# A one-core block of attention-like mixing and a gated network: TensorE makes 53 unread products in the waits of the first two groups

## The chip, the cores and the metric

The kernel runs on one core of a Trainium2 chip. The metric is the device time of one execution, in microseconds (us); lower is better. TensorE (PE) multiplies, VectorE (DVE), ScalarE (ACT) and GpSimd (POOL) work elementwise, SyncE (SP) issues transfers.

## What is computed

The input `x` has 32 sequences of 256 tokens with 128 channels, in f32. Each token row is normalized; then comes a block with two halves, and then a feed-forward network, each with a normalization behind it and a residual:

```python
x = x + _layernorm(_L0_attn_ref(_layernorm(x), ...))
x = x + _layernorm(_L0_ffn_ref(_layernorm(x), ...))

# _L0_attn_ref
x = x + lif(time_mix(layer_norm(x, ln1_s, ln1_b), ...))
x = x + lif(channel_mix(layer_norm(x, ln2_s, ln2_b), ...))
# time_mix: mixes each token with the one before, k = xk @ Wk, v = xv @ Wv,
#   sigmoid(xr @ Wr) * wkv(w_decay, u_first, k, v) @ Wo     (wkv: a scan over time)
# channel_mix: sigmoid(xr @ Wr) * (square(relu(xk @ Wk)) @ Wv)     (Wk 128x512, Wv 512x128)
# lif: a scan over time that emits spikes where a voltage reaches 1
# _L0_ffn_ref: h = silu(x @ w1) * (x @ w2); h = gelu(h @ h1); h = gelu(h @ h2); h @ w3
```

The weights of the feed-forward network are -1, 0 and 1 with a scale for each output.

## The kernel before

The 32 sequences are cut into 16 groups of two, 512 tokens each. A group is held with tokens on the partitions for normalizations and turned on TensorE to channels on the partitions for products and scans over time. Each engine has an instruction stream of its own, written out by hand as *turns*. In turn i the engines work on several groups at once: on group i the input norm, on i-1 the time mix, on i-2 its output and the channel mix, on i-3 and i-4 the feed-forward network. `g[k]` in the code is group i-k, and `on[k]` says whether there is one. Turns below 3 run `first_turn`, those from 3 on `turn`, the last ones `last_turn`; turns 6 to 13 are a loop. Engines wait for each other by semaphores, and an engine never runs ahead of an instruction of its own that waits.

On TensorE a group passes these steps (the names are those of the code and of the text below):

- `turn_1` transposes the normalized tokens (`n1`) into the bank `p_turn`; ScalarE makes `z1` of it, GpSimd the difference `d1`, VectorE the three inputs `mixed1`.
- `k_product`, `r_product_1`, `v_product`: f32 products of 512 columns. VectorE scans `p_k` (`maximum`, `excess`), ScalarE takes exponentials, VectorE and GpSimd scan and multiply, and at the end VectorE writes `yr`.
- `out_product` multiplies `yr` with Wo; ScalarE copies it to `h_in[0]`, VectorE scans the voltage and marks spikes, `fired_sum(0)` asks whether any neuron fired, GpSimd branches on it, `spikes_turned(0)` transposes the spikes back.
- `turn_2` transposes the second norm (`n2`); ScalarE makes `z2`, GpSimd `d2`, VectorE `mixed2`. Then `r_product`, `channel_k` 0 to 3 (ScalarE: `relu`, `square`) and `channel_v` 0 to 3. Behind `r_product` ScalarE takes tanh and loads the table of exponentials, then comes `relu` 0.
- `channel_v` 3 ends the channel mix; VectorE makes `h_in[1]` of it and scans it, and then come `fired_sum(1)` and `spikes_turned(1)`.
- `turn_4`, `to_gate`, `to_value`, `hidden` and `last_product` are the feed-forward network, whose weights are split into a rounded part `w_hi` and a rest `w_lo`.

TensorE's program exists twice from turn 3 on: with products of `w_lo`, and without them where all of `w_lo` is 0. At the end of turn 2 TensorE sums the maxima of the rest (`rest_sum`), VectorE copies the sum to `w_rest_all`, and TensorE reads it and branches:

```python
program(False, last=2)
...
long_weights = pe.value_load(w_rest_all[0:1, 0:1].bitcast(I32))
with pe.If(long_weights != 0):
    program(True, first=3)
with pe.Else():
    program(False, first=3)
```

The weights of the mixes lie in `mix`, blocks 0 to 2 being Wk, Wv and Wr; the third transfer that SP issues brings blocks 0 to 4 (`s_mix_in`), and the next one brings `kk`, 1 MB of the other weights. `p_f` are two banks for results of the feed-forward network; before that network starts, `p_f[1]` holds the scales of w3 (until `s_w3_scaled`), and `p_f[0]` receives `rest_sum`.

Of the kernel before, what the change touches and what calls it, by code (L numbers as in the profile page):

```python
# [31 lines left out]
P = 128  # L32
# [39 lines left out]
def build(nc, x_in, vec_in, scale_in, mix_in, ffn_in, out):  # L72
# [13 lines left out]
    with ExitStack() as ctx:  # L86
# [1348 lines left out]
        def _(pe):  # L1435
# [3 lines left out]
            def program(general, **turns):  # L1439
# [5 lines left out]
                def turn_1(g):  # L1445
                    pe.wait_ge(s_n[1], g.n + 1)
                    after(pe, s_f_out, g.n - 4)
                    if isinstance(g.n, int):
                        after(pe, s_f0_lo, g.n - 3)
                        after(pe, s_z2, g.n - 2)  # L1450
                        after(pe, s_z1, g.n - 1)
                    turned(1, g, n1)

                def turn_2(g):
                    pe.wait_ge(s_n[2], g.n + 1)
                    after(pe, s_z1, g.n + 1)
                    if isinstance(g.n, int):
                        after(pe, s_f_out, g.n - 3)
                        after(pe, s_f0_lo, g.n - 2)
                        after(pe, s_z2, g.n - 1)  # L1460
                    turned(2, g, n2)
# [17 lines left out]
                def k_product(g):  # L1479

                    after(pe, s_h_in[0], g.n - 1)
                    if isinstance(g.n, int):
                        after(pe, s_e, g.n - 1)
                    time_product(g, 0, "Wk", p_k, s_k)
# [21 lines left out]
                def out_product(g):  # L1506

                    after(pe, s_e, g.n)
                    if isinstance(g.n, int):
                        after(pe, s_h_in[0], g.n - 1)  # L1510
                    pe.wait_ge(s_yr, g.n + 1)
                    if isinstance(g.n, int) and g.n == 0:
                        pe.wait_ge(s_quarter[0], 1)
                    pe.matmul(p_k[:, :], mix[:, MIX["Wo"]], flat(yr[:, :, :]), start=True, stop=True).then_inc(s_wo, 1)

                def fired_sum(k, g):

                    if k == 0:
                        after(pe, s_fired_all[1], g.n - 1)
                        if isinstance(g.n, int):  # L1520
                            after(pe, s_h_in[1], g.n - 1)
                            after(pe, s_relu, g.n - 1, HB, 3)
                            after(pe, s_relu, g.n - 1, HB, 1)
                            after(pe, s_tanh_r, g.n)
                            after(pe, s_fired_all[0], g.n - 1)
                    elif k == 1:
                        after(pe, s_h_in[1], g.n)
                        if isinstance(g.n, int):
                            after(pe, s_relu, g.n, HB, 3)
                            after(pe, s_relu, g.n, HB, 1)  # L1530
                            after(pe, s_tanh_r, g.n + 1)
                            after(pe, s_fired_all[0], g.n)
                            after(pe, s_fired_all[1], g.n - 1)
                    pe.wait_ge(s_fired[k], g.n + 1)
                    pe.matmul(p_m[0][:, 2 * k:2 * k + 1], ones16[:, :], fired[k][:, :], start=True,
                              stop=True).then_inc(s_fired_sum[k], 1)

                def spikes_turned(k, g):

                    if k == 0:  # L1540
                        after(pe, s_x3, g.n - 1)
                        if isinstance(g.n, int):
                            after(pe, s_x2, g.n - 1)
                    elif k == 1:
                        after(pe, s_x2, g.n)
                        if isinstance(g.n, int):
                            after(pe, s_x3, g.n - 1)
                    pe.wait_ge(s_spikes[k], g.n + 1)
                    tile = flat(spikes[k][:, :, :])
                    for j in range(J):  # L1550
                        last = pe.transpose(p_spk[:, k, j * P:(j + 1) * P], tile[:, j * P:(j + 1) * P], ident16[:, :])
                    last.then_inc(s_spk_tok[k], 1)
# [229 lines left out]
                def last_product(g):  # L1782
# [10 lines left out]
                                             start=(m == 0), stop=(m == HB - 1))  # L1793
                    last.then_inc(s_w3, 1)

                def rest_sum():

                    pe.wait_ge(s_rest1, 1)
                    pe.matmul(p_f[0][:, 0:1], ones16[:, :], w_rest1[:, :], start=True,
                              stop=True).then_inc(s_rest_sum, 1)  # L1800

                def first_turn(g, on):

                    if on[2]:
                        out_product(g[2])
                        fired_sum(0, g[2])
                        spikes_turned(0, g[2])
                    if on[1]:
                        k_product(g[1])
                    if on[2]:  # L1810
                        turn_2(g[2])
                    if on[1]:
                        r_product_1(g[1])
                    if on[2]:
                        r_product(g[2])
                    if on[1]:
                        v_product(g[1])
                    if on[2]:
                        channel_k(g[2], 0)
                        channel_k(g[2], 1)  # L1820
                        channel_k(g[2], 2)
                        channel_v(g[2], 0)
                        channel_k(g[2], 3)
                        channel_v(g[2], 1)
                        channel_v(g[2], 2)
                    if on[0]:
                        turn_1(g[0])
                    if g[0].n == 2:
                        rest_sum()

                def turn(g, on):

                    if on[4]:
                        to_gate(g[4], 3)
                        to_value(g[4], 3)
                    if on[3]:
                        channel_v(g[3], 3)
                    if on[2]:
                        out_product(g[2])
                    if on[4]:  # L1840
                        hidden(1, g[4], 0)
                        hidden(1, g[4], 1)
                    if on[3]:
                        fired_sum(1, g[3])
                    if on[4]:
                        hidden(1, g[4], 2)
                    if on[3]:
                        spikes_turned(1, g[3])
                    if on[2]:
                        fired_sum(0, g[2])  # L1850
                    if on[4]:
                        hidden(1, g[4], 3)
                    if on[2]:
                        spikes_turned(0, g[2])
                    if on[1]:
                        k_product(g[1])
                    if on[4]:
                        hidden(2, g[4], 0)
                        hidden(2, g[4], 1)
                        hidden(2, g[4], 2)  # L1860
                    if on[2]:
                        turn_2(g[2])
                    if on[1]:
                        r_product_1(g[1])
                    if on[4]:
                        hidden(2, g[4], 3)
                    if on[2]:
                        r_product(g[2])
                    if on[1]:
                        v_product(g[1])  # L1870
                    if on[2]:
                        channel_k(g[2], 0)
                    if on[3]:
                        turn_4(g[3])
                    if on[2]:
                        channel_k(g[2], 1)
                        channel_k(g[2], 2)
                    if on[4]:
                        last_product(g[4])
                    if on[3]:  # L1880
                        to_gate(g[3], 0)
                    if on[2]:
                        channel_v(g[2], 0)
                        channel_k(g[2], 3)
                    if on[3]:
                        to_value(g[3], 0)
                        to_gate(g[3], 1)
                    if on[2]:
                        channel_v(g[2], 1)
                        channel_v(g[2], 2)  # L1890
                    if on[3]:
                        to_value(g[3], 1)
                        to_gate(g[3], 2)
                    if on[0]:
                        turn_1(g[0])
                    if on[3]:
                        to_value(g[3], 2)
# [115 lines left out]
```

## Time and profile before

| | |
|---|---|
| median of 3 runs | 709.31 us (706.81 to 709.71) |
| profiled execution | 710.65 us |
| its span | 708.5 us |
| mean granted clock of TensorE | 0.949 |
| TensorE busy | 613.5 us (87%), 2563 products |
| VectorE, ScalarE, GpSimd busy | 566.3, 482.4, 438.4 us |
| TensorE's longest waits up to 100 us | 15.0 us in 4 for `n` (L1442), 11.0 in 1 for `yr`, 5.3 in 1 with the releaser "issue" |

The span is the time from the first to the last instruction of the profiled execution; the device time holds 2.15 us more. Busy time counts products on TensorE and no weight loads; products overlap in the pipeline, so ends of products are later than the start of the next. The granted clock is 1.00 at full speed (2.4 GHz) and 0.50 at half (1.2 GHz). A row names engine, line of the kernel, operation and its tiles, output first. A product of f32 operands stands as two instructions.

### The profile page before, as it was taken

To read this page: it belongs to the slowest core of one execution; us is meant where nothing else is said; L and a number is where in the kernel's file an instruction comes from. 1 tells how busy PE (TensorE), PEld (TensorE's weight loads), DVE (VectorE), ACT (ScalarE), POOL (GpSimd) and SP (SyncE) were. 2 spreads that over 40 slices of the span, in tenths; PEclk is the share of its full clock that TensorE was granted. 3 is DMA by queue.
4 is the path that set the end of the run, shared out by engine and by line. 5 is a ranking of instruction groups with operands and counts; after the bars stand their busy time and mean duration, and the time that the engine had idled before them with its cause. 6 is when DMAs were issued, how large, how long until landed. Compare 5 with 4: busy or idle time off the path is not lost. (4 is left out here: it accounts for less than half of the span.)

```text
span 708.5 us, 10945 instructions
## 1 busy us (share of the span) xinstructions
PE 613.5 (87%) x2563; PEld 399.0 (56%) x2563; DVE 566.3 (80%) x1552; ACT 482.4 (68%) x718; POOL 438.4 (62%) x560
## 2 busy tenths in 40 slices
PE   1245589999999999999999999999999999999884
PEld 0012236666656566666666666656666666566753
DVE  3866779898989999998989898989889897936230
ACT  3636076877869595959687786959595968757261
POOL 4333454687877767676768677786767684635242
PEclk9758579999999999999999999999999999999897
DMA  7000000001010000001010101000000101000000
GB/s 271 23 8 16 1 15 17 16 15 31 16 31 17 30 16 12 18 15 30 15 30 15 30 15 30 15 30 16 17 15 1 30 1 31 16 0 16 1 15 16
DMA packets 26538, 16.82 MB, mean 24 GB/s; under 512 B 1152, under 2 KB 25728, under 8 KB 26240
## 3 DMA queue, kind: packets, MB, share of 16 engines
q1 hardware_dynamic: 26496, 16.34, 7.6%
q8 instruction: 17, 0.28, 0.2%
q14 instruction: 25, 0.20, 0.1%
HBM read 12.14 MB, written 4.19 MB: 23 GB/s over the span
## 5 line engine op out<-in xcount | busy, mean ns | idle before, releaser
L735 ACT ACTIVATE hid<-p_f,scale 128x512 f32<-128x512 f32 x128 | 86.6, 687 | 102.0 <-PE p_f L1634 101.7
L1634 PE MATMUL p_f<-b_lo,w_hi 128*128 128x512 f32 x256 | 114.0, 445 | 11.0 <-DVE b_lo L306 10.9
L1634 PE MATMUL p_f<-a_lo,w_hi 128*128 128x512 f32 x256 | 112.5, 440 | 2.8 <-DVE a_lo L306 1.0
L449 POOL TENSOR_TENSOR nd<-factors,pq 128x512 f32<-128x512 f32 x32 | 38.0, 1187 | 102.1 <-DVE pq L1065 102.1
L1634 PE MATMUL p_f<-a_hi,w_hi 128*128 128x512 f32 x256 | 101.0, 394 | 0.0
L1634 PE MATMUL p_f<-b_hi,w_hi 128*128 128x512 f32 x256 | 101.0, 394 | 0.0
L433 POOL TENSOR_TENSOR rstd<-var,minus_half 128x4 f32<-128x4 f32 x64 | 75.0, 1172 | 2.5
L1619 PE MATMUL p_m<-kk,mix 128*128 128x512 f32 x128 | 64.0, 602 | 9.5 <-issue 5.3
L1634 PEld LDWEIGHTS p_f<-b_lo,w_hi 128*128 128x128 f32 x256 | 48.1, 188 | 37.5 <-issue 25.7
L1792 PEld LDWEIGHTS p_turn<-w,hid 128*128 128x128 f32 x512 | 61.5, 200 | 12.3 <-DVE f_lo L1173 11.0
L1792 PE MATMUL p_turn<-w,hid 128*128 128x128 f32 x512 | 63.9, 285 | 2.3 <-DVE f_lo L1173 1.4
L420 POOL TENSOR_TENSOR var<-mv,eps_row 128x4 f32<-128x4 f32 x64 | 35.0, 547 | 48.4 <-DVE mv L985 48.3
L1603 PE MATMUL p_m<-mixed,mix 128*128 128x512 f32 x128 | 63.6, 600 | 0.0
L1634 PEld LDWEIGHTS p_f<-a_lo,w_hi 128*128 128x128 f32 x256 | 48.2, 188 | 27.0 <-issue 8.6
L1634 PEld LDWEIGHTS p_f<-b_hi,w_hi 128*128 128x128 f32 x256 | 48.2, 188 | 15.0 <-issue 6.2
L441 POOL TENSOR_SCALAR f_out<-f_out,neg_mean,rstd 128x128 f32<-128x128 f32 x64 | 55.0, 871 | 0.8 <-POOL rstd L433 0.8
L1634 PEld LDWEIGHTS p_f<-a_hi,w_hi 128*128 128x128 f32 x256 | 48.3, 189 | 11.2 <-issue 3.6
L1094 DVE TENSOR_TENSOR_SCAN volt<-half_row,h_in 128x256 f32<-128x256 f32 x64 | 50.4, 827 | 2.8 <-ACT h_in L686 2.8
L1442 PE MATMUL p_turn<-ident,n 128*128 128x128 f32 x192 | 31.0, 286 | 16.6 <-DVE n L1001 16.5
L729 ACT ACTIVATE a_hi<-hid 128x512 fp32r<-128x512 f32 x64 | 40.6, 635 | 6.8 <-DVE hid L1184 6.2
L441 POOL TENSOR_SCALAR x<-xa,neg_mean,rstd 128x128 f32<-128x128 f32 x64 | 45.0, 712 | 0.3 <-POOL rstd L429 0.2
L1442 PEld LDWEIGHTS p_turn<-ident,n 128*128 128x128 f32 x192 | 23.3, 145 | 36.6 <-DVE n L1001 31.8
(135 smaller groups left out, 1506.8 us busy)
## 6 DMA issues: line engine op xcount, KB each, us to landing
xa<-in_x SPq DMA_DIRECT2D x16, 256.0 KB, 2.9
xb<-in_x SPq DMA_DIRECT2D x16, 256.0 KB, 2.9
out<-y_out SPq DMA_DIRECT2D x16, 256.0 KB, 3.0
kk<-in_ffn SPq DMA_DIRECT2D x1, 1024.0 KB, 7.1
hid<-in_ffn SPq DMA_DIRECT2D x1, 1024.0 KB, 9.6
mix<-in_mix SPq DMA_DIRECT2D x1, 512.0 KB, 6.5
gate<-in_ffn SPq DMA_DIRECT2D x1, 512.0 KB, 5.6
mix<-in_mix SPq DMA_DIRECT2D x1, 320.0 KB, 3.8
```

The costliest lines, as they stand in the source:

```text
L420: pool.tensor_tensor(var[n][:, :], mv[n][:, :, 1], eps_row[:, :], ALU.add).then_inc(s_var[n], 1)
L433: pool.tensor_tensor(rstds[n][:, :], var[n][:, :], minus_half[:, 0], ALU.pow).then_inc(s_rstd[n], 1)
L441: last = pool.tensor_scalar(out_[:, j], in_[:, j], neg_mean[n][:, j:j + 1], rstd[:, j:j + 1], ALU.add, ALU.mult)
L449: pool.tensor_tensor(nd[:, n], factors[:, 0], pq[:, n, :, 0:T], ALU.mult).then_inc(s_apq, 1)
L729: act.activation(dst[:, m], hid[:, m], ACT.Copy).then_inc(s_hi[layer], 1)
L735: act.activation(hid[:, m], p_f[m % 2][:, :], ACT.Gelu, scale=scale[:, 1 + layer, m:m + 1]).then_inc(s_gelu[layer], 1)
L1094: last = dve.tensor_tensor_scan(volt[k][:, b], half_row[:, :], h_in[k][:, b], 0.0, ALU.mult, ALU.add)
L1442: last = pe.transpose(p_turn[:, j * P:(j + 1) * P], tiles[:, j], ident[:, :])
L1603: pe.matmul(p_m[m % 2][:, :], mix[:, MIX["fWk"] + m], flat(mixed2[:, 1]), start=True, stop=True).then_inc(s_fk, 1)
L1619: last = pe.matmul(p_m[0][:, :], mix[:, MIX["fWv"] + m], kk[:, m], start=(m == 0), stop=(m == HB - 1))
L1634: last = pe.matmul(out_, w[:, b], x[:, k], start=(k == 0 and t == 0), stop=(k == n - 1 and t == len(terms) - 1))
L1792: last = pe.matmul(p_turn[:, j * P:(j + 1) * P], hid[:, m, j * P:(j + 1) * P], w3[:, m], start=(m == 0), stop=(m == HB - 1))
```

## The change

A new helper `busy` makes products of the weights with themselves into a bank of `p_f` that nobody reads at that time, 384 columns each, for groups 0 and 1 alone, at fourteen places of `first_turn` and `turn`. It waits for the weights, and in turn 3 and later also for the scaling of w3. No other engine is touched, and no result depends on these products.

```diff
+                def busy(g, counts, k):
+
+                    if isinstance(g.n, int) and g.n in counts:
+                        pe.wait_ge(s_mix_in, 16)
+                        if k:
+                            pe.wait_ge(s_w3_scaled, 1)
+                        for _ in range(counts[g.n]):
+                            pe.matmul(p_f[k][:, 0:3 * P], mix[:, 0], flat(mix[:, 0:3]), start=True, stop=True)
...
                 def first_turn(g, on):
 
                     if on[2]:
+                        busy(g[2], {0: 15}, 0)
                         out_product(g[2])
+                        busy(g[2], {0: 3}, 0)
                         fired_sum(0, g[2])
+                        busy(g[2], {0: 1}, 0)
                         spikes_turned(0, g[2])
                     if on[1]:
+                        busy(g[1], {0: 7}, 0)
                         k_product(g[1])
                     if on[2]:
+                        busy(g[2], {0: 5}, 0)
                         turn_2(g[2])
...
                     if on[2]:
+                        busy(g[2], {0: 1}, 0)
                         r_product(g[2])
...
                         channel_k(g[2], 2)
+                        busy(g[2], {0: 2}, 0)
                         channel_v(g[2], 0)
...
                     if on[0]:
+                        busy(g[0], {1: 3}, 0)
                         turn_1(g[0])
...
                     if on[3]:
+                        busy(g[3], {0: 6}, 1)
                         channel_v(g[3], 3)
...
                     if on[3]:
+                        busy(g[3], {0: 1}, 1)
                         fired_sum(1, g[3])
...
                     if on[3]:
+                        busy(g[3], {0: 2}, 1)
                         spikes_turned(1, g[3])
...
                     if on[2]:
+                        busy(g[2], {1: 1}, 1)
                         spikes_turned(0, g[2])
...
                     if on[2]:
+                        busy(g[2], {1: 5}, 1)
                         turn_2(g[2])
...
                     if on[2]:
+                        busy(g[2], {1: 1}, 1)
                         r_product(g[2])
```

What this makes of TensorE's order at the start, from the first `k_product` (L1476, `p_k`) to the first `out_product` (L1514). L1803 is the unread product, and a row with x7 stands for seven in a row; the lines below the helper move down by 9.

```order
+L1803 MATMUL p_f<-mix 128x384 x7
 L1476 MATMUL p_k<-mixed,mix 128x512
 L1476 MATMUL p_m<-mixed,mix 128x512
 L1476 MATMUL p_v<-mixed,mix 128x512
-L1442 MATMUL p_turn<-ident,n 128x128 x4
+L1803 MATMUL p_f<-mix 128x384 x3
+L1442 MATMUL p_turn<-ident,n 128x128 x4
+L1803 MATMUL p_f<-mix 128x384 x15
 L1514 MATMUL p_k<-yr,mix 128x512
```

Seven unread products now stand between group 0's first transposes and its k product, three ahead of the transposes of group 1, and fifteen ahead of the output product; the order of all others is as before.

The second place is the end of turn 2 and the start of turn 3, in group 0. L1799 (now L1808) is `rest_sum`, the next two rows load the flag and branch on it, L1619 is `channel_v` 3 and L1514 the output product of group 1.

```order
-L1799 MATMUL p_f<-w_rest,ones 128x1
-L1974 TENSOR_LOAD w_rest_all
-L1975 COMPARE_AND_BRANCH
+L1808 MATMUL p_f<-w_rest,ones 128x1
+L1997 TENSOR_LOAD w_rest_all
+L1998 COMPARE_AND_BRANCH
+L1803 MATMUL p_f<-mix 128x384 x6
 L1619 MATMUL p_m<-kk,mix 128x512
 L1514 MATMUL p_k<-yr,mix 128x512
```

The six unread products stand behind the branch, at the head of the code that it jumps to, and ahead of `channel_v` 3.

## Rows read from the trace of the kernel before

**Rows 1.** The page: TensorE's granted clock in 40 slices, in tenths.

```profile
PEclk9758579999999999999999999999999999999897
```

**Rows 2.** Stretches: us; busy us of PE, PEld, DVE, ACT, POOL; clock; DMA; GB/s.

```profile
65.50:100.00 34.50, 17.09 (x41) 7.28 (x40) 24.77 (x76) 12.22 (x18) 14.73 (x21) 0.65 0.06 17
...
130.00:650.00 520.00, 499.04 (x2165) 329.69 (x2166) 457.54 (x1250) 393.27 (x595) 360.55 (x443) 1.00 0.06 18
```

**Rows 3.** Timeline of TensorE: start us, us, engine, line, operation, [idle before <-releaser].

```profile
10.12 1.11 PE L1442 MATMUL p_turn<-ident,n 128*128 128x128 f32 x4 [4.17 <-DVE n L1001]
16.35 2.07 PE L1476 MATMUL p_k<-mixed,mix 128*128 128x512 f32 x2 [5.12 <-DVE mixed L1021]
18.21 1.91 PE L1476 MATMUL p_m<-mixed,mix 128*128 128x512 f32 x2
19.92 1.91 PE L1476 MATMUL p_v<-mixed,mix 128*128 128x512 f32 x2
24.52 0.66 PE L1442 MATMUL p_turn<-ident,n 128*128 128x128 f32 x4 [2.69 <-DVE n L1001]
36.19 2.04 PE L1514 MATMUL p_k<-yr,mix 128*128 128x512 f32 x2 [11.01 <-DVE yr L1088]
41.05 0.16 PE L1535 MATMUL p_m<-fired,ones 128*128 128x1 bf16 x1 [2.82 <-DVE spikes L1102]
42.64 0.61 PE L1551 MATMUL p_spk<-ident,spikes 128*128 128x128 bf16 x4 [1.43 <-POOLq L488]
...
48.86 1.12 PE L1442 MATMUL p_turn<-ident,n 128*128 128x128 f32 x4 [3.80 <-DVE n L1001]
...
52.75 2.07 PE L1565 MATMUL p_m<-mixed,mix 128*128 128x512 f32 x2 [1.07 <-DVE mixed L1139]
...
70.86 2.04 PE L1619 MATMUL p_m<-kk,mix 128*128 128x512 f32 x2 [5.32 <-issue]
...
90.77 2.05 PE L1565 MATMUL p_m<-mixed,mix 128*128 128x512 f32 x2 [1.35 <-DVE mixed L1139]
```

**Rows 4.** The same timeline where the granted clock is full.

```profile
62.37 1.02 PE L1603 MATMUL p_m<-mixed,mix 128*128 128x512 f32 x2
63.22 1.88 PE L1619 MATMUL p_m<-kk,mix 128*128 128x512 f32 x4
64.94 0.60 PE L1442 MATMUL p_turn<-ident,n 128*128 128x128 f32 x4
```

**Rows 5.** Short stretches, columns as in rows 2: where the clock changes.

```profile
56.20:56.30 0.10, 0.10 (x1) 0.00 (x0) 0.10 (x2) 0.10 (x1) 0.00 (x0) 0.55 0.00 0
93.80:94.00 0.20, 0.20 (x1) 0.00 (x1) 0.20 (x3) 0.20 (x1) 0.20 (x1) 0.91 0.00 0
100.00:105.00 5.00, 5.00 (x11) 2.66 (x10) 3.49 (x10) 3.95 (x7) 2.88 (x3) 0.66 0.00 0
```

**Rows 6.** Timeline of ScalarE and VectorE up to group 0's relu.

```profile
9.44 1.91 ACT L626 ACTIVATE w_hi<-kk 128x2048 fp32r<-128x2048 f32 x1 [5.39 <-DMA kk<-in_ffn]
...
18.45 1.26 DVE L1028 TENSOR_TENSOR_SCAN o<-decay_row,p_k 128x256 f32<-128x256 f32 x2 [0.84 <-PE p_k L1476]
...
55.48 1.28 ACT L657 ACT_TABLE_LOAD   x1
...
57.37 0.60 ACT L704 ACTIVATE kk<-p_m 128x512 f32<-128x512 f32 x1 [0.61 <-PE p_m L1603]
```

**Rows 7.** TensorE's queue at the branch, and the copy of the flag before it.

```profile
65.61 0.15 DVE L1114 COPY w_rest_all<-p_f 1x1 f32<-1x1 f32 x1 [0.21 <-PE p_f L1799]
...
L1975 PEldq COMPARE_BRANCH  x1: 4246/4246/4246, 66.4 to 66.4; - x1
```

**Rows 8.** Timeline of VectorE, GpSimd and ScalarE in group 1.

```profile
75.58 1.27 DVE L1094 TENSOR_TENSOR_SCAN volt<-half_row,h_in 128x256 f32<-128x256 f32 x2
...
88.61 1.04 POOL L459 TENSOR_TENSOR d<-z 128x512 f32<-128x512 f32 x1
...
95.14 0.60 ACT L704 ACTIVATE kk<-p_m 128x512 f32<-128x512 f32 x1 [0.39 <-PE p_m L1603]
```

## The prediction

> **What bounds the kernel now.** I read the page first, then the stretches, then the timeline of the first 105 us. The page's clock line [rows 1] shows TensorE's granted clock well below full speed in slices 2 to 6 (17.7 us each), and full from there almost to the end. The stretches [rows 2] show why: from 130 to 650 us TensorE is busy 499 of 520 us, while from 65.5 to 100 us it is busy 17.1 of 34.5 us at a mean clock of 0.65. So the middle is set by TensorE, and the start by a chain in which the engines hand one group of 512 tokens to each other. An edit of the start is worth what it moves the point at which TensorE stops waiting; the middle carries this shift to the end.
>
> The timeline shows what a product costs at either level. Two f32 products of 512 columns that follow each other start 1.71 us apart in the cold part (18.21 and 19.92 in [rows 3]) and 0.85 us apart at full clock (62.37 and 63.22 in [rows 4]): 1.2 and 2.4 GHz. One by itself ends after 2.04 to 2.07 us, or after 1.02. (The clock view says 1.00 before 25.5 us, where it has recorded no change yet; I go by the durations, which there are those of 1.2 GHz.) An unread product has 384 columns, three quarters: **1.28 us at 1.2 GHz, 0.64 at 2.4**, one behind the other.
>
> How soon does the clock rise? In the unbroken run from 52.75 it came up at 56.25 [rows 3, 5], 3.5 us in; in the run from 90.77 at about 93.8, 3.05 us in [rows 3, 5]; in the run from 16.35 to 21.83 not within 5.5 us, though the transposes at 24.52 took 0.66 us instead of 1.11 [rows 3]. Call c the time at 1.2 GHz after such a run begins: n unread products take 0.64n + c/2. I take c = 4.5, the middle, with ends 3.1 and 5.5, and "not at all" as the outer one.
>
> **The change, step by step.** Nothing is removed. 37 unread products go into group 0's waits and 16 into the next stretch, 53 by the order of instructions. They matter by what they delay and by the clock.
>
> *Seven ahead of the first k product.* TensorE is free at about 11.2 and waits until 16.35 [rows 3]. The weights that they read don't hold them: the load queued behind that one on SP had landed by 9.44 [rows 6]. They need 4.48 + 2.25 = 6.7 us, end at 17.9, and the k product starts 1.6 late. It then takes 1.02 instead of 2.07, so its result is late by 0.5 (-0.15 at c = 3.1, +1.0 at c = 5.5). VectorE's scan at 18.45 waits for it [rows 6], and from there DVE, ACT and POOL pass the work on until yr, which releases the product at 36.19 [rows 3]. Term: **+0.5**.
>
> *Three and fifteen more.* The fifteen need 9.6 us at 2.4 GHz and lie in a wait of 11.0 (before 36.19 in [rows 3]); cover enough unless the clock drops in the wait before them. Term: 0; with a drop 9.6 + 2.25 = 11.85, so up to 0.9 late.
>
> *Group 0's products at 2.4 GHz.* The next small ones (3, 1, 5, 1) need 1.9, 0.6, 3.2 and 0.6 us and lie in waits of 2.8, 1.4, 3.8 and 1.1 [rows 3]: nothing. What they keep up is the clock, and four operations on the chain shrink: the output product at 36.19 by 1.0, the transposed spikes at 42.64 by some 0.2 (an estimate, a third of 0.61), the transposes at 48.86 from 1.12 to 0.60 [rows 3, 4], so 0.5. The channel's first product, at 52.75, then starts at 52.75 + 0.5 - 1.7 = 51.55. Before, the ACT table load behind it ended at 56.76, 4.01 us after its start, and relu at 57.37 still waited 0.61 for TensorE's channel_k [rows 6]. With this product 1.05 shorter the table is in 2.96 us after its start, at 54.5; channel_k ends after 0.85 + 0.85 + 1.02 = 2.7 us, at 54.3. So relu moves from 57.37 to 54.5: **-2.9** after group 0.
>
> *The six behind the branch.* Here the wait isn't what it looks like. TensorE idles until 70.86, released by "issue", not by an operand [rows 3]. The row of the branch shows why: DVE copies the flag at 65.61, and COMPARE_BRANCH holds TensorE's queue for 4246 ns from 66.4, to 70.65 [rows 7]. The six products stand behind that branch in the program, so they can't fill its wait; they start when it ends, and channel_v stands behind them. The branch moves with the chain, to an end at 68.0. After 5 us of nothing the clock is down, as it was before (the product at 70.86 took 2.04). Six products take 3.84 + 2.25 = 6.1 us; channel_v starts at 74.1 and ends at 2.4 GHz at 75.1, against 72.90 before: **+2.2** (+1.5 at c = 3.1; all six at 1.2 GHz take 7.7, which gives +3.8).
>
> A rule against the row: the Trainium skill (Advanced Engine Details and Errata, Control Flow Timing) gives a compare-and-branch about 108 ns, and another of its pages (Runtime: NRT & Kernel Launch, Instruction fetch mechanics) says that a taken branch to a target beyond the fetched instructions stalls until they are fetched. The 4246 ns agree with the second and not with the first; by the first the branch would end 4.1 us sooner in both kernels and the six would cost the same, behind it.
>
> *Group 1.* From channel_v's end DVE works without a pause to the second voltage scan at 75.58 [rows 8], so all of it arrives there. Two sets of transposed spikes give back 0.2 each: +1.8. The small groups (1, 2, 1, 5, 1) fit into their waits. The transposes at 86.59 would be 0.5 shorter, but the shift at 88.61 stands behind POOL's earlier work and not behind them [rows 8]: 0. The channel's product moves from 90.77 to 92.6; again the table is in 2.96 later, at 95.5, where relu began at 95.14 [rows 8]: **+0.4**.
>
> *After that* the same rows follow. In the kernel before the clock sank once more, to a mean of 0.66 in 100 to 105 us [rows 5]. I cost this at nothing either way, since silu and relu of that stretch, on ACT, wait for its own chain; if TensorE is what sets it, up to 1.7 us hang on it, in either kernel.
>
> Sum: +0.5 - 1.7 - 1.7 + (2.2 + 2.9) - 0.4 - 1.4, which is +0.4. (The second -1.7 is the shorter channel product and the 0.61 of waiting for channel_k; the -1.4 is the same in group 1; the bracket is 6.1 us of products less 1.0 for channel_v.) The profiled execution took 710.65 us, 2.15 of it around the span: 711.05. It lies 1.34 above the median of 709.31, so the median should be **709.7**.
>
> The Trainium skill (TensorE: Matmul & The Clock Gate, What's actually happening) puts the whole ramp penalty below 1% of a typical kernel's span; that would cap any gain here at 7.1 us. The rows agree: all that TensorE runs cold on the chain is worth less.
>
> **Rivals.**
> 1. *The six products are hidden*, because the branch's wait or something later swallows them. Then channel_v starts at 68.0 and ends at 69.0, 3.9 earlier than before; 0.4 for the spikes, and relu of group 1 at 90.77 - 4.3 + 2.96 = 89.4, so -5.7: 703.6. For it: a wait of 5.3 us stands there, and later slack on TensorE isn't excluded. Against it: the row of the branch, and that no operand is named as releaser of the product at 70.86. The Trainium skill's advice (TensorE: Matmul & The Clock Gate, Why this matters for your kernels) to leave TensorE no long gaps points this way.
> 2. *The clock rises at once behind the branch.* Then the six take 3.84, channel_v ends as before, and relu comes at 90.37 + 2.96 = 93.3: -1.8, 707.5. Against it: no run of products in the rows rose within 3 us.
> 3. *The clock rises late at both dense places* (slower). It decides from about c = 7 on. All seven at 1.2 GHz take 8.96, the k product stays cold, +3.8; less 1.7; relu at 57.8, +0.4. The branch ends at 71.3, six at 1.2 GHz take 7.7, channel_v cold ends at 81.0, +8.1; relu of group 1 at 98.5 + 2.96, +6.3: 715.6. For it: the 5.5 us from 16.35. Against it: the two rises after 3 to 3.5 us.
> 4. *Unread products don't raise the clock.* Then all 53 run at 1.2 GHz and overrun their waits by 3.8, 8.2, 1.0, 2.6, 7.7, 0.8 and 2.1, about 26 us: 736. Against it: they are the same kind of f32 product as those under which it rose.
>
> **How the numbers follow.** The forecast, within its bounds, has 0.70: c = 3.1 at both places gives -0.95, a late rise of the second +2.5, and three runs of before already differ by 2.9 us, so its own range is 707 to 713. Rival 1 has 0.12, rival 2 0.04, rival 3 0.11, rival 4 0.03. What this measurement can tell from no change is about 0.5%, 3.5 us: faster 0.12, same 0.74, slower 0.14. The range 706.6 to 713.2 leaves out the rivals 1, 3 and 4 for the most part.
>
> **What the profile after would show.** Right: the k product starts at 17 to 18.5; the output product takes 1.02; relu of group 0 comes near 54.5; COMPARE_BRANCH takes over 4 us, and six unread products start within 0.3 us of its end, the first ones 1.28 apart; channel_v starts 5.4 to 7.7 us behind it; relu of group 1 near 95.5. Wrong: a branch row that overlaps these products, or unread products still 1.28 apart in the wait ahead of the output product. The forecast fails most easily in c, which counts at both dense places, and in whether the clock holds through the idle 2 us between them.

## The result: 0.46% slower, by the six products behind the branch

The changed kernel takes 710.97 us (median of 9 runs, 709.72 to 712.33), the kernel before 707.66 (9 runs, 706.47 to 709.71). The ratio is 1.0046, with a 95% interval of 1.0031 to 1.0061: 3.3 us slower, inside the forecast range and below what I had called a difference from no change, but clear of the noise of nine runs. The forecast was +0.4 us. Its 709.7 us lie within 1.3 us of the measured median by luck: they start from the median of the first three runs of before (709.31), and nine runs gave 707.66. The profiled execution after has a span of 709.9 us.

The page of the changed kernel, which answers to [rows 1]: busy time and share of TensorE, and its clock in 40 slices.

```profile
PE 640.7 (90%) x2669; PEld 415.6 (59%) x2669; DVE 566.2 (80%) x1552; ACT 482.7 (68%) x718; POOL 437.2 (62%) x560
...
PEclk9998999999999999999999999999999999999998
```

The change did what its words say: the clock is near full in the slices where it was at 5 to 8 tenths. The unread products stand in the busy time, 640.7 instead of 613.5 us, and say nothing about speed. The stretches, which answer to [rows 2]:

```profile
65.50:100.00 34.50, 25.57 (x69) 12.19 (x69) 20.26 (x63) 6.90 (x10) 12.87 (x18) 0.85 0.03 10
...
130.00:650.00 520.00, 498.92 (x2163) 329.09 (x2162) 458.82 (x1257) 393.84 (x596) 360.14 (x443) 1.00 0.06 19
```

From 65.5 to 100 us TensorE is busy 25.6 instead of 17.1 us at a mean clock of 0.85 instead of 0.65; the middle is as before, 498.9 of 520 us. Next, the timeline of TensorE, answering to [rows 3]; L1803 is the unread product, two instructions for each.

```profile
10.99 7.08 PE L1803 MATMUL p_f<-mix 128*128 128x384 f32 x14
17.91 1.02 PE L1476 MATMUL p_k<-mixed,mix 128*128 128x512 f32 x2
...
25.52 11.54 PE L1803 MATMUL p_f<-mix 128*128 128x384 f32 x30
36.90 1.02 PE L1514 MATMUL p_k<-yr,mix 128*128 128x512 f32 x2
...
48.35 0.65 PE L1442 MATMUL p_turn<-ident,n 128*128 128x128 f32 x4 [1.48 <-DVE n L1001]
...
51.78 1.13 PE L1565 MATMUL p_m<-mixed,mix 128*128 128x512 f32 x2 [0.94 <-DVE mixed L1139]
...
68.10 7.01 PE L1803 MATMUL p_f<-mix 128*128 128x384 f32 x12 [5.08 <-issue]
74.94 1.02 PE L1619 MATMUL p_m<-kk,mix 128*128 128x512 f32 x2
...
93.54 1.27 PE L1565 MATMUL p_m<-mixed,mix 128*128 128x512 f32 x2 [2.02 <-DVE mixed L1139]
94.60 1.92 PE L1476 MATMUL p_v<-mixed,mix 128*128 128x512 f32 x2
```

The seven begin at 10.99, end at about 17.9 and push the k product from 16.35 to 17.91; it takes 1.02 us. The fifteen fill the wait ahead of the output product to its end (36.90), which then takes 1.02 instead of 2.04. The six begin at 68.10, and channel_v stands behind them at 74.94. At 93.54 the channel's first product of group 1 meets a clock that falls: it takes 1.27, and the v product behind it 1.92. The queue of TensorE at the branch, answering to [rows 7], min/median/max in ns and its start:

```profile
L1998 PEldq COMPARE_BRANCH  x1: 3998/3998/3998, 63.9 to 63.9; - x1
```

It ends at 67.9, and the six start 0.2 us later. The two relu on ScalarE that end the steps of the forecast, answering to [rows 6, 8]:

```profile
54.85 0.60 ACT L704 ACTIVATE kk<-p_m 128x512 f32<-128x512 f32 x1
...
98.08 0.60 ACT L704 ACTIVATE kk<-p_m 128x512 f32<-128x512 f32 x1 [1.34 <-PE p_m L1603]
```

Group 0 gained 2.5 us here (57.37 to 54.85), group 1 lost 2.9 (95.14 to 98.08). What this is worth at the end can be read off all profiled executions. The columns are starts of relu 0 of either group, the branch's end, the span, and the span less relu of group 1:

| kernel | relu, group 0 | branch ends | relu, group 1 | span | difference |
|---|---|---|---|---|---|
| before | 57.37 | 70.6 | 95.14 | 708.5 | 613.4 |
| before, second profile | 57.04 | 69.8 | 94.63 | 706.2 | 611.6 |
| changed | 54.85 | 67.9 | 98.08 | 709.9 | 611.8 |
| changed, second | 53.19 | 65.9 | 95.78 | 707.6 | 611.8 |
| changed, third | 53.48 | 66.5 | 96.28 | 708.2 | 611.9 |
| without the six | 54.16 | 66.9 | 89.72 | 701.1 | 611.4 |
| only the six | 57.45 | 70.8 | 98.42 | 710.0 | 611.6 |
| seven ahead of the branch | 52.99 | 65.6 | 88.26 | 699.8 | 611.5 |
| twelve behind it | 54.71 | 67.8 | 101.75 | 713.1 | 611.4 |
| group 0 alone | 54.25 | 67.3 | 90.40 | 702.0 | 611.6 |
| four first | 52.42 | 64.9 | 87.80 | 699.9 | 612.1 |
| four ahead of the branch | 54.26 | 67.0 | 90.61 | 702.5 | 611.9 |
| four and four | 52.46 | 65.3 | 87.24 | 698.9 | 611.7 |
| the same, two more | 52.80 | 65.5 | 87.39 | 697.9 | 610.5 |

In twelve of fourteen the rest of the kernel took 611.4 to 612.1 us: what happens up to relu of group 1 arrives at the end in full. The two others differ by the clock at the end of the kernel: a set of transposed products (L1792) there took 6.78 us in the first profile of before, 5.3 to 5.5 in the twelve, and 3.84 in the last kernel. No added product stands there; why the clock differs there is not shown.

### The profile page after: what moved, and what is told of

It is laid out like the page before. It is cut to its first block and busy times, and to the rows that moved or that the text cites. A ratio compares the mean times of both kernels' runs of the same rounds, so it can differ in the third digit from the quotient of the medians.

```text
span 709.9 us, 11163 instructions
## 1 busy us (share of the span) xinstructions
PE 640.7 (90%) x2669; PEld 415.6 (59%) x2669; DVE 566.2 (80%) x1552; ACT 482.7 (68%) x718; POOL 437.2 (62%) x560
## 5 line engine op out<-in xcount | busy, mean ns | idle before, releaser
L1792 PEld LDWEIGHTS p_turn<-w,hid 128*128 128x128 f32 x512 | 60.1, 196 | 12.8 <-DVE f_lo L1173 11.5
L1619 PE MATMUL p_m<-kk,mix 128*128 128x512 f32 x128 | 62.9, 593 | 2.9 <-ACT kk L704 2.9
L1792 PE MATMUL p_turn<-w,hid 128*128 128x128 f32 x512 | 62.8, 282 | 2.3 <-DVE f_lo L1173 1.4
L1803 PE MATMUL p_f<-mix 128*128 128x384 f32 x106 | 43.8, 563 | 5.1 <-issue 5.1
L729 ACT ACTIVATE b_hi<-hid 128x512 fp32r<-128x512 f32 x64 | 40.5, 632 | 2.0
```

Of the source, the lines that this page charges most:

```text
L729: act.activation(dst[:, m], hid[:, m], ACT.Copy).then_inc(s_hi[layer], 1)
L1619: last = pe.matmul(p_m[0][:, :], mix[:, MIX["fWv"] + m], kk[:, m], start=(m == 0), stop=(m == HB - 1))
L1792: last = pe.matmul(p_turn[:, j * P:(j + 1) * P], hid[:, m, j * P:(j + 1) * P], w3[:, m], start=(m == 0), stop=(m == HB - 1))
L1803: pe.matmul(p_f[k][:, 0:3 * P], mix[:, 0], flat(mix[:, 0:3]), start=True, stop=True)
```

## The experiments

Each kernel is compared with the kernel before on the same chip; the timed ones ran 6 to 12 times. The median of before was 707.39 us beside the first four, 706.86 beside the next four (group 0 alone, four first, four ahead, four and four) and 708.11 beside the last one and the three further profiles, so ratios compare across these and medians don't.

**Without the six.** One line of the changed kernel goes:

```diff
                     if on[3]:
-                        busy(g[3], {0: 6}, 1)
                         channel_v(g[3], 3)
```

> The changed kernel without the six unread products behind the branch; the other 47 stay. Theory (the six stand behind the branch and are pure delay, 6.8 us of products less about 1 us for the faster channel_v): the branch ends near 68.1 us, channel_v starts there, takes 2.04 us at 1.2 GHz and ends near 70.1 instead of 76.0. The small groups behind it then run cold and give back 1 to 2 us, so relu of group 1 comes 4 to 5 us earlier than the 98.1 of the changed kernel, near 93.5: about 706.5 us, ratio to before 0.995 to 1.000. Rival (the six are hidden, and the loss comes from the seven ahead of the k product or from the small groups): no change against the changed kernel, 711 us, ratio 1.0046.

Measured: 702.55 us against 707.39, ratio 0.9933 (0.9912 to 0.9954). Its timeline of TensorE behind the branch, and the branch:

```profile
67.07 2.05 PE L1619 MATMUL p_m<-kk,mix 128*128 128x512 f32 x2 [4.74 <-issue]
68.91 1.91 PE L1514 MATMUL p_k<-yr,mix 128*128 128x512 f32 x2
...
86.68 1.10 PE L1565 MATMUL p_m<-mixed,mix 128*128 128x512 f32 x2 [0.33 <-DVE mixed L1139]
```

```profile
L1997 PEldq COMPARE_BRANCH  x1: 3670/3670/3670, 63.2 to 63.2; - x1
```

channel_v starts at 67.07, 0.2 us behind the branch's end, and takes 2.05 at 1.2 GHz. Even so relu of group 1 comes at 89.72, 3.8 us sooner than I expected: from the branch's end to relu it takes 22.8 us, with the six 30.2. The difference of 7.4 is the 6.84 of the products, less 1.0 for the faster channel_v, plus 1.5: here the channel's first product (86.68) ran at full clock and relu followed in 3.04 us, in the changed kernel in 4.54. The theory stands; I had set its gain too low, and the ratio lies below the 0.995 to 1.000 that I expected.

**Only the six**, in the kernel before: the reverse, all other calls of `busy` removed.

```diff
-                        busy(g[2], {0: 15}, 0)
                         out_product(g[2])
-                        busy(g[2], {0: 3}, 0)
                         fired_sum(0, g[2])
...
                         busy(g[3], {0: 6}, 1)
                         channel_v(g[3], 3)
```

> The kernel before with the six unread products behind the branch alone. Theory: group 0 is as before, the branch ends near 70.7, the six take 6.1 to 7.7 us, channel_v ends 4 to 5.5 us later than the 72.9 of before, and the warmer clock behind it gives back 0.5 to 1.5 us: +3 to +5 us, near 711.7, ratio 1.004 to 1.007. Rival (the six are hidden): 707.7, ratio 1.000.

Measured: 711.63 us, ratio 1.0070 (1.0043 to 1.0098). TensorE behind the branch:

```profile
70.96 5.69 PE L1803 MATMUL p_f<-mix 128*128 128x384 f32 x12 [5.34 <-issue]
76.49 1.02 PE L1619 MATMUL p_m<-kk,mix 128*128 128x512 f32 x2
...
95.38 1.10 PE L1565 MATMUL p_m<-mixed,mix 128*128 128x512 f32 x2 [1.35 <-DVE mixed L1139]
```

The six take 5.53 us from 70.96 to 76.49, and channel_v ends at 77.5, 4.6 later than in [rows 3]. They alone make the kernel slower by at least as much as the whole change does; the two intervals overlap.

The same six cost less here than in the changed kernel. From the branch's end to relu of group 1 it takes 27.6 us with them and 24.5 and 24.8 in the two profiles of before, about 3 more; in the changed kernel it takes 29.8 to 30.2, and 22.8 without them, about 7 more. The cost is not a fixed one: here the channel's first product (95.38) still ran at full clock, 1.10 us, and relu followed in 3.04, while in the changed kernel the clock was falling or low there.

**Twelve behind the branch.**

```diff
-                        busy(g[3], {0: 6}, 1)
+                        busy(g[3], {0: 12}, 1)
```

> The changed kernel with twelve instead of six behind the branch. Theory (pure delay at full clock for each further product): 6 x 0.64 = 3.84 us more, 714.8 us, ratio to before 1.010. Rival (a wait swallows them up to some number): less than 1 us more.

Measured: 714.32 us, ratio 1.0090 (1.0063 to 1.0118).

```profile
67.90 10.73 PE L1803 MATMUL p_f<-mix 128*128 128x384 f32 x24 [5.02 <-issue]
78.47 1.02 PE L1619 MATMUL p_m<-kk,mix 128*128 128x512 f32 x2
```

Twelve take 10.57 us, 3.73 more than six, and relu of group 1 comes 3.67 later. The ratio goes from 1.0046 to 1.0090, which is 3.1 us; the two intervals just stay apart. No wait swallows any.

**Seven ahead of the branch**, none behind it:

```diff
                     if g[0].n == 2:
                         rest_sum()
+                        busy(g[0], {2: 7}, 1)
...
-                        busy(g[3], {0: 6}, 1)
                         channel_v(g[3], 3)
```

> The changed kernel, but the six behind the branch replaced by seven right ahead of it, after the sum of the flag. Theory (the branch holds TensorE's queue of instructions, not the array, so that products issued before it run meanwhile): the seven take 4.5 us from 62.9 to 67.4, COMPARE_BRANCH still ends near 68.1, channel_v and the output product start there at full clock; against the changed kernel channel_v ends 6.9 us earlier, relu of group 1 near 91 to 92: about 704.5 us, ratio 0.994 to 0.997. Rival (the load of the flag waits until the array is empty, so that the products delay the branch): the branch ends at about 72.5 and channel_v starts 1 to 2 us later than that of before, which gives 710 to 711 us.

Measured: 703.25 us, ratio 0.9951 (0.9935 to 0.9967). The timeline, the branch, and two stretches (columns as in [rows 2]):

```profile
61.02 4.76 PE L1803 MATMUL p_f<-mix 128*128 128x384 f32 x14
65.76 1.10 PE L1619 MATMUL p_m<-kk,mix 128*128 128x512 f32 x2
68.65 1.02 PE L1514 MATMUL p_k<-yr,mix 128*128 128x512 f32 x2 [1.79 <-issue]
```

```profile
L1998 PEldq COMPARE_BRANCH  x1: 3498/3498/3498, 62.1 to 62.1; - x1
```

```profile
66.00:67.00 1.00, 0.86 (x2) 0.22 (x2) 0.11 (x1) 0.00 (x0) 0.00 (x0) 1.00 0.05 16
67.00:68.00 1.00, 0.00 (x0) 0.00 (x0) 0.97 (x2) 0.00 (x0) 0.00 (x0) 1.00 0.00 0
```

The seven run from 61.0 to 65.8 while the branch, from 62.1, holds the queue of instructions to 65.6: this branch stops the issue and not the array. So this wait can be filled, from its other side. channel_v starts at once and at full clock. But the output product behind it starts only at 68.65, with the releaser "issue", though its operand `yr` had been written by 64.6, and a queue of instructions fetches 16 KB from 66 to 67 us. I read this as TensorE being out of instructions. VectorE's second voltage scan waited for this product, until 70.33, and the gain of the faster channel_v was gone. From the branch's end to relu it takes 22.7 us, as without the seven, and the intervals of the two ratios overlap.

**Four ahead of the branch** instead of seven, to move this edge.

```diff
-                        busy(g[0], {2: 7}, 1)
+                        busy(g[0], {2: 4}, 1)
```

> As the run with seven products right ahead of the branch, with four. In that run the output product behind channel_v started only 2.9 us after it, with the releaser issue, while 16 KB of instructions were being fetched. Theory (the fetch of the next block of instructions stalls TensorE's queue, and 12 instructions fewer move the edge of the block behind the output product): the output product follows channel_v within 0.9 us at full clock, h_in of group 1 comes 1.8 us sooner relative to the branch's end, relu of group 1 at 21 us behind the branch's end instead of 22.7: near 701.5 us, ratio 0.990 to 0.993. Rival (the stall comes a fixed time after the branch whatever stands there): the output product still starts 3 us after the branch's end, 703.

Measured: 704.46 us, ratio 0.9951 (0.9933 to 0.9970), not better than seven and outside the 0.990 to 0.993 expected.

```profile
67.19 1.10 PE L1619 MATMUL p_m<-kk,mix 128*128 128x512 f32 x2 [2.08 <-issue]
68.12 1.02 PE L1514 MATMUL p_k<-yr,mix 128*128 128x512 f32 x2
...
85.85 2.05 PE L1565 MATMUL p_m<-mixed,mix 128*128 128x512 f32 x2 [1.18 <-DVE mixed L1139]
```

The output product now follows channel_v in 0.93 us, so the stall went with the 12 instructions (a product is two MATMUL and two LDWEIGHTS in the trace). But the channel's first product (85.85) took 2.05 us, and relu came 4.8 us behind it: the clock had fallen there, as in the changed kernel. That the stall goes is shown. What it was worth can be read from the branch's end to the start of the channel's first product: 19.6 us with seven, 18.9 here, and 18.9 and 18.8 in the last two kernels, so some 0.8 us, and the clock took more than that here.

**Group 0 alone**: the 37 products of turns 1 and 2, none from turn 3 on.

```diff
-                        busy(g[3], {0: 6}, 1)
                         channel_v(g[3], 3)
...
-                        busy(g[3], {0: 1}, 1)
                         fired_sum(1, g[3])
...
-                        busy(g[3], {0: 2}, 1)
                         spikes_turned(1, g[3])
...
-                        busy(g[2], {1: 1}, 1)
                         spikes_turned(0, g[2])
...
-                        busy(g[2], {1: 5}, 1)
                         turn_2(g[2])
...
-                        busy(g[2], {1: 1}, 1)
                         r_product(g[2])
```

> The changed kernel with the unread products of turns 1 and 2 alone (37), none from the branch on. Theory: group 0 gains as in the changed kernel (relu of group 0 near 54.5, branch end near 67.5), and from the branch on everything is cold as in the kernel before, where relu of group 1 came 24.5 us after the branch's end, against 22.85 without the six but with the small groups. So relu of group 1 near 92, 3 us earlier than before: about 704.2 us, ratio 0.994 to 0.997. Rival (the gain of the run without the six comes from the small groups of group 1): ratio 0.999 to 1.000.

Measured: 703.71 us, ratio 0.9945 (0.9930 to 0.9961), as expected. The small groups from turn 3 on are worth nothing that this can tell: without the six and with them the ratio was 0.9933, and the intervals overlap.

**Four ahead of the first k product** instead of seven, none behind the branch.

```diff
-                        busy(g[1], {0: 7}, 0)
+                        busy(g[1], {0: 4}, 0)
...
-                        busy(g[3], {0: 6}, 1)
```

> The changed kernel without the six behind the branch, and with four instead of seven ahead of the first k product. Theory (seven overrun their wait by 1.6 us, of which the faster k product gives back 1.05): four take at most 5.1 us from 11.0, end by 16.1, the k product starts at 16.35 as before and, with the clock up by then or soon, ends 0.5 to 1.0 us sooner than with seven: 702.0 us, ratio to before 0.991 to 0.993. Rival (three products less, and the clock comes up later or falls sooner): the k product at 16.35 still takes 2.0 us, and nothing is gained or lost against seven, 702.5.

Measured: 703.22 us, ratio 0.9941 (0.9925 to 0.9957).

```profile
10.99 4.89 PE L1803 MATMUL p_f<-mix 128*128 128x384 f32 x8
15.72 1.02 PE L1476 MATMUL p_k<-mixed,mix 128*128 128x512 f32 x2
```

The four end at 15.72, the k product starts there and takes 1.02. The ratio lies outside the 0.991 to 0.993 expected. With four, relu of group 0 came at 52.42, 52.46 and 52.80 in three kernels, with seven between 52.99 and 54.85 in eight profiles.

VectorE's `mixed1`, the operand of the k product, itself starts between 14.17 and 15.57 us in the fourteen profiles, so the step is read better from that start to the start of `yr`. It is 19.8 us in the three profiles with nothing ahead of the k product, 19.3 to 20.9 with seven (20.2 on average) and 18.8 to 19.2 with four (19.0). By this four are 1.2 us better than seven and 0.8 better than none, while seven lose 0.4 on average. The ratios, 0.9941 here and 0.9933 with seven, don't show it.

**Four and four**: four ahead of the k product, four ahead of the branch, none behind it.

```diff
-                        busy(g[1], {0: 7}, 0)
+                        busy(g[1], {0: 4}, 0)
...
                         rest_sum()
+                        busy(g[0], {2: 4}, 1)
...
-                        busy(g[3], {0: 6}, 1)
```

> Both: four ahead of the first k product and four right ahead of the branch, none behind it. Theory: the two gains add, 701 us, ratio 0.989 to 0.992. Rival (the clock falls in the gaps that the smaller groups leave): no better than 702.5, the run without the six.

Measured: 702.39 us, ratio 0.9927 (0.9906 to 0.9949), just outside the 0.989 to 0.992 expected. Relu of group 1 comes at 87.24, but the intervals of this kernel and of the one without the six overlap; that the gains add isn't shown.

**The same with two more** (three instead of one), to hold the clock in the wait ahead of the channel's first product of group 1:

```diff
                     if on[2]:
-                        busy(g[2], {1: 1}, 1)
+                        busy(g[2], {1: 3}, 1)
                         r_product(g[2])
```

> Four ahead of the k product, four ahead of the branch, none behind it, and three instead of one in the wait ahead of the channel's first product of group 1. Theory (in the changed kernel the clock fell at 94.4 us because TensorE was nearly idle in the 4 us ahead of that product; it then took 4.5 us from its start to relu instead of 2.96): relu follows in 2.9 to 3.1 us here, relu of group 1 at 87 us or sooner, about 702 us, ratio 0.991 to 0.994. Rival (it was chance, or the products overrun the wait): the channel's product starts later than 20.6 us behind the branch's end, or relu is still over 3.5 us behind it.

Measured: 699.94 us against 708.11, ratio 0.9893 (0.9868 to 0.9918), the lowest of all and faster than both kernels; its interval overlaps that of four and four. The channel's first product of group 1, and the end of the kernel:

```profile
84.34 1.10 PE L1565 MATMUL p_m<-mixed,mix 128*128 128x512 f32 x2 [0.73 <-DVE mixed L1139]
85.28 1.02 PE L1476 MATMUL p_v<-mixed,mix 128*128 128x512 f32 x2
```

```profile
656.82 3.84 PE L1792 MATMUL p_turn<-w,hid 128*128 128x128 f32 x32 [1.41 <-DVE f_lo L1173]
```

The product takes 1.10, relu follows it at 87.39, in 3.05 us, and the product starts 18.8 us behind the branch's end: the theory's numbers. But these numbers don't show that the two added products did it. With one product in that wait, four and four has the same (84.19, 1.10 us, relu 21.9 us behind the branch's end as here), and so has four first:

```profile
80.79 1.92 PE L1476 MATMUL p_m<-mixed,mix 128*128 128x512 f32 x2
...
84.19 1.10 PE L1565 MATMUL p_m<-mixed,mix 128*128 128x512 f32 x2 [0.33 <-DVE mixed L1139]
```

```profile
80.58 0.66 PE L1442 MATMUL p_turn<-ident,n 128*128 128x128 f32 x4 [2.06 <-DVE n L1001]
81.07 1.02 PE L1476 MATMUL p_m<-mixed,mix 128*128 128x512 f32 x2
...
84.75 1.10 PE L1565 MATMUL p_m<-mixed,mix 128*128 128x512 f32 x2 [2.01 <-DVE mixed L1139]
```

In four and four the clock had fallen before the product at 80.79 (1.92 us) and was back at 84.19; in four first it held through both waits of 2 us. Where the clock falls decides, and that differs between kernels with the same small groups. Of this profile's gain another 1.1 us lie behind relu (610.5 instead of 611.6), where L1792 took 3.84 us; whether that comes with the edit is not shown.

**Three further profiles**, of the changed kernel twice and of the kernel before once, without an edit.

> The changed kernel once more, for the spread of its profile. Theory (what was off in the forecast is the size of the clock's terms, and they differ from one execution to the next): the first seven end between 16.5 and 18.5 us, the six behind the branch take 5.4 to 7.7 us, relu of group 1 lies between 95 and 99, and the span is relu of group 1 plus 611.6 us, within 0.5. Rival (a fixed cost of the change that the forecast left out): all of it within 0.3 us of the first profile, relu at 98.1.

> A third profile of the changed kernel. The same as for the second: by the theory the six take 5.4 to 7.7 us and relu of group 1 comes between 95 and 99; by the rival it is 98.1 again.

> The kernel before once more. Theory (its first profile, 710.65 us, was 3 us above the median of nine because the clock fell near the end, where the last transposed products at 664 us took 6.8 instead of 5.5 us): the span is relu of group 1 plus 611.6 if the clock holds there, 613.4 if it falls, and relu of group 1 lies between 94.5 and 97. Rival (the end always costs this): plus 613.4 again.

Measured: 709.43, 710.21 and 708.25 us, one execution each. TensorE in the two of the changed kernel: the six, channel_v, the last products ahead of the channel's first product of group 1, and that product:

```profile
66.05 6.58 PE L1803 MATMUL p_f<-mix 128*128 128x384 f32 x12 [4.68 <-issue]
72.47 1.02 PE L1619 MATMUL p_m<-kk,mix 128*128 128x512 f32 x2
...
86.88 0.66 PE L1442 MATMUL p_turn<-ident,n 128*128 128x128 f32 x4 [2.06 <-DVE n L1001]
87.37 1.27 PE L1476 MATMUL p_m<-mixed,mix 128*128 128x512 f32 x2
88.44 1.48 PE L1803 MATMUL p_f<-mix 128*128 128x384 f32 x2
91.05 2.04 PE L1565 MATMUL p_m<-mixed,mix 128*128 128x512 f32 x2 [1.13 <-DVE mixed L1139]
```

```profile
66.60 6.52 PE L1803 MATMUL p_f<-mix 128*128 128x384 f32 x12 [4.94 <-issue]
72.95 1.02 PE L1619 MATMUL p_m<-kk,mix 128*128 128x512 f32 x2
...
91.54 2.05 PE L1565 MATMUL p_m<-mixed,mix 128*128 128x512 f32 x2 [1.17 <-DVE mixed L1139]
```

The seven ended at 16.5 and 16.6 instead of 17.9, the six took 6.42 and 6.35 instead of 6.84, relu came at 95.78 and 96.28 instead of 98.1. So these sizes do differ by execution. But one thing doesn't: the channel's first product of group 1 met the falling or low clock in all three (1.27, 2.04, 2.05 us), and relu came 4.54, 4.73 and 4.74 us behind it, where the forecast had 2.96. In the first profile the clock fell at about 94.4, under this product and behind a second wait; in the two others it fell at 88.0 and 88.5, in the work between the two waits (the product at 87.37 took 1.27 instead of 1.02, the unread one at 88.44 took 1.48 instead of 0.81). In the second profile of before the span was relu plus 611.6, so the end doesn't always cost 613.4.

## Why the prediction came out as it did

*Seven ahead of the k product*: forecast +0.5, k product at 17.9. Right in the first profile, 17.91; in the two others it started at 16.47 and 16.59, below the 17 to 18.5 that I had named as a sign of being right.

*Three and fifteen more, at nothing*: nearly right, with the case I had given up to 0.9 us for. The timeline has 11.5 us for the fifteen, and the output product starts where they end, at 36.90 instead of 36.19. Of this 0.7 us 0.5 are the late k product, so the fifteen cost 0.2.

*Group 0 at 2.4 GHz, -2.9 in all*: relu at 54.85 against 54.5 forecast in the first profile, 53.2 and 53.5 in the others; table load and not channel_k sets it. Right.

*The six behind the branch, +2.2*: right in its mechanism, which three kernels show (without, alone, doubled), and a little small: 6.84, 6.42 and 6.35 us against 6.1. COMPARE_BRANCH took 3.4 to 4.3 us in all kernels, never near 0.1 (under 4 us in all three profiles of the changed kernel, where I had written over 4), and the six never began before its end. Rival 1 (hidden) and rival 2 (the clock up at once) are out; so is rival 4, since the clock rose under the unread products at both dense places, and rival 3, since the seven ended at 17.9 us or sooner.

*Group 1, from the channel's product to relu*: this is the step that went most wrong, in size. I wrote "The channel's product moves from 90.77 to 92.6; again the table is in 2.96 later". That took the clock of group 1 for held because each small group fitted its wait. It was 4.5 to 4.7. Ahead of this product TensorE has two waits of 2 us with 2 us of work between them, since the product waits for POOL and not for the transposes, and the clock fell in each of three profiles, once behind the second wait and twice behind the first. Two sentences above I had named POOL's work myself, and used it only to cost the transposes at nothing. The waits alone don't decide it, since four first has the same two and kept its clock. The term is -1.4 in the forecast, and with 1.6 to 1.8 taken off it becomes about +0.3. My last sentence had named this risk, whether the clock holds; no bound of the sum had it.

In the first profile the sum closes with these two sizes. The branch ended at 67.9 (forecast 68.0), channel_v began 0.8 us later than forecast (74.94 for 74.1), the channel's product 0.9 (93.54 for 92.6) and relu 2.6 (98.08 for 95.5): 0.9 for the six and 1.6 behind the channel's product make +2.9 out of +0.4. In the two other profiles the seven ended 1.3 and 1.4 us sooner, and with that relu came at 95.78 and 96.28.

What is open is the median. In the profiled executions relu of group 1 is 1.8 us later than before on average (96.7 of three, 94.9 of two), while the medians differ by 3.3; the profiles of before, 710.65 and 708.25, lie above their median of 707.66, two of three of the changed kernel below theirs. So few profiles can't say which part of the clock's chances is typical.

*After that, nothing*: right. The clock's drop from 100 to 105 us in the kernel before [rows 5] is absent in the first profile of the changed one and in the second of before, and present in the two others of the changed one; the rest takes 611.6 to 611.9 us in all four. The 613.4 us of the first profile of before, which the forecast carried along, lies for 1.4 us of the difference in L1792 near the end (6.78 instead of 5.4).

*The bound of 7.1 us on any gain*: open. The last kernel gained 1.1%, 0.8 to 1.3%, which is 5.8 to 9.3 us, so the runs neither keep to the bound nor break it clearly.

## What to carry to other kernels

Here a filler paid only in a wait that ends with an operand. Where the releaser is the queue itself ("issue", a branch), what was written behind it came on top of the wait, at the clock that the idle time had left; written ahead of it, it ran meanwhile. And a clock that fillers hold up must be followed through every wait, the ones that they don't shorten too. The same kernel went from 0.46% slower to 0.7% faster when the six behind the branch were removed; that is shown. Three fewer at the head, four ahead of the branch and two more in group 1 took it to 1.1%, but the intervals of these two kernels overlap, so the worth of these three edits is not shown by the times.

## What I had not expected of the hardware

The branch of TensorE stops only the issue: seven products ran from 61.0 to 65.8 us while COMPARE_BRANCH stood from 62.1 to 65.6.

Behind the branch there is a second stall that the kernel before doesn't show: with 7 products of four instructions each ahead of the branch the output product started 2.9 us behind channel_v while 16 KB were fetched, and with 4 of them 0.93 us behind it. The Trainium skill (Runtime: NRT & Kernel Launch, Instruction fetch mechanics) says that instructions are refilled in blocks of 16 KiB and that a taken branch breaks the fetch ahead; the 16 KB of that microsecond agree. But 16 KB are fetched shortly behind the branch in the other kernels too, without such a stall: before from 71.0 to 71.5 us with the branch's end at 70.6, four ahead from 68.0 to 68.5 with its end at 67.0. The view doesn't say which engine they are for. That the stall goes with 12 instructions less is shown; that the fetch causes it is argued.
